# Expert stage of a routed feed-forward kernel: eight hidden chunks between ScalarE and VectorE, results scattered by halves, products of two-expert tiles laid between another tile's long ones

## The chip, the cores and the metric

One core of one Trainium2 chip runs the whole program. The metric is the device time of one execution in microseconds (us). The kernel before was timed in three runs: 1258.9, 1256.6 and 1252.9 us, median 1256.6 us.

## The reference, cut to what matters

The input is 2 images of 256 channels, 56 by 56 pixels, so 6272 tokens of 256 numbers. First comes neighbourhood attention, which this change does not touch. Then every token goes through two of eight experts:

```python
t = _to_tokens(x)
# t + ffn(layernorm(t))
gate_logits = xf @ Wg + bg
top_w, top_i = jax.lax.top_k(gate_logits, 2)
top_w = softmax(top_w)
for e in range(8):
    h = gelu(xf @ W1[e] + b1[e])          # 256 -> 1024, exact gelu
    out = out + w_dense[:, e:e+1] * (h @ W2[e] + b2[e])   # 1024 -> 256
```

So there are 12544 pairs of token and expert, each with a product of 256 by 1024, a gelu, a product of 1024 by 256, a bias, a weight (the gate), and a sum into the output row of the token.

## The kernel before, in words

Stages before the experts compute the attention, the layer norm and the routing, and write every token's normalised row (as two float16 halves of a float32 number, with its output row number and its gate numbers behind) into an expert-sorted table `slots` in HBM. The weights W1 and W2 lie in SBUF as float16 pairs (high part and rest), `w1s` and `w2s`.

The expert stage (`stage_e`) works through NT = 53 tiles of ST = 256 rows. Tiles 0 to 45 and 50 to 52 belong to one expert each. Tiles 46 to 49 (`halves`) are two half tiles of HT = 128 rows, with an expert for each half. Tiles 0 to 43 (`LOOPED` = 44, four tiles a turn, U = 4) run in a loop on each engine, the rest is written out. All engines follow their own program and meet by semaphores:

- **SyncE** (L1493 to L1516) loads the rows of tile m into `xg[m % 4]`, one transfer of 273 KB (two for a tile of halves). From tile 4 on it waits for `xg_free`.
- **TensorE** (L1578 to L1676) has three steps. `turn(m)` transposes the 256 rows of tile m by eight matmuls of 128 columns into `ps_x`, and waits for the load of the tile. `up(m)` makes the eight chunks (HC = 8) of 128 hidden units: six matmuls each with 256 columns, because of the two parts of row and weight. Chunk hc goes to `ps_h[hc % 4]`. `up_halves(m)` does the same for tiles 46 to 49 with twelve matmuls of 128 columns a chunk, six for each half. `down(m)` makes the result of each half of the rows from all eight chunks: 24 matmuls of 256 columns for half 0 and then 24 for half 1, into `ps_y[m % 2]`. The order is up(m+1), turn(m+2), down(m), and so on.
- **ScalarE** (L1679 to L1697) takes each hidden chunk from `ps_h` through the gelu into `gf[hc % 4]`, float32, and raises `g_ok`. For tiles of halves these are two instructions a chunk, since the bias differs.
- **VectorE** (L1758 to L1790) splits each chunk (`split`): a cast into `g_hi` and a subtraction into `g_lo`, which raises `gs_ok`. Then `take_x(m)` copies the transposed rows from `ps_x` to `xt` (L1751) and makes the differences for the gate (L1754). Then `take_y(m)` moves the result of both halves from PSUM to `y_f` with bias (L1788, L1783). The order is split(n+1), take_x(n+2), take_y(n).
- **GpSimd** (L1519 to L1575) makes the gate (`weigh`, four small instructions, each waited for, L1524 to L1535), and in `send(n)` waits for `yf_ok` (L1540) and for the transfers of the tile before (`y_done`, L1543), raises `xg_free` (L1544), multiplies both halves by the gate (L1546, two instructions of 256 columns), waits for them (L1549), and scatters each half with adding into the output by an indirect DMA of its own (L1554).

What paces TensorE inside `up`: chunk hc may start only when the chunk four before it has been split, so from hc = 4 on it waits for VectorE's work on the same tile:

```python
pe.wait_ge(gs_ok, hc - 3 + (0 if first else HC))
```

Load of tile n+3 waits for the `xg_free` that `send(n)` raises; `turn(n+3)` on TensorE follows `up(n+2)`, which begins just when `down(n)` ends.

Of the kernel before, what the change touches and what calls it, by code (L numbers as in the profile page):

```python
# [6 lines left out]
F32 = mybir.dt.float32  # L7
# [4 lines left out]
ALU = mybir.AluOpType  # L12
# [1411 lines left out]
def stage_e(nc, slots_dram, out, w1s, w2s, keep, tc, cf):  # L1424


    with ExitStack() as c:
# [9 lines left out]
        halves = range(PAIR0, PAIR0 + PAIRS)  # L1437
        id_e, b1_sb, b2_sb = keep["id"], keep["b1"], keep["b2"]
# [3 lines left out]
        gf = sb("e_gf", [128, 4, ST], F32)  # L1442
# [25 lines left out]
        xg_f = xg[:, :, :, :].bitcast(F32)  # L1468

# [20 lines left out]
        with nc.Block() as block:  # L1490
# [28 lines left out]
            def _(pool):  # L1519
# [58 lines left out]
            def _(pe):  # L1578
# [11 lines left out]
                def up(m, e, first):  # L1590
# [4 lines left out]
                    for hc in range(HC):  # L1595
                        if not first or hc >= 4:
                            pe.wait_ge(gs_ok, hc - 3 + (0 if first else HC))
                        n = 0
                        for k in range(KC):
                            for w, p in ((0, 0), (0, 1), (1, 0)):  # L1600
                                a = k * FH + hc * 128
                                mm = pe.matmul(ps_h[:, hc % 4, 0:ST],  # L1602
                                               w1s[:, bass.ds(e, 1), w, a:a + 128].rearrange("p a n -> p (a n)"),
# [6 lines left out]
                def up_halves(m, experts):  # L1610
# [3 lines left out]
                    pe.sem_inc(xt_ok, -1)  # L1614
                    for hc in range(HC):
                        pe.wait_ge(gs_ok, hc - 3 + HC)
                        for h, e in enumerate(experts):
                            n = 0
                            for k in range(KC):
                                for w, p in ((0, 0), (0, 1), (1, 0)):  # L1620
                                    a = k * FH + hc * 128
                                    mm = pe.matmul(ps_h[:, hc % 4, h * HT:(h + 1) * HT],
# [4 lines left out]
                    pe.sem_inc(gs_ok, -HC)  # L1627

                def down(m, experts):
                    s = m % 2  # L1630
                    for h in range(2):
                        n = 0
                        for hc in range(HC):
                            for g, w in ((g_hi, 0), (g_hi, 1), (g_lo, 0)):
                                a = hc * C
                                mm = pe.matmul(ps_y[:, s, h * C:(h + 1) * C], g[:, s, hc, h * 128:(h + 1) * 128],  # L1636
                                               w2s[:, bass.ds(experts[h], 1), w, a:a + C].rearrange("p a n -> p (a n)"),
                                               start=n == 0, stop=n == 3 * HC - 1)
                                n += 1
                    mm.then_inc(y_ok, 1)  # L1640
# [10 lines left out]
                with pe.Fori(0, LOOPED // U) as i:  # L1651
                    e = expert(U * i)
                    for j in range(U):
                        after = expert(U * i + j + 1)
                        up(j + 1, after, False)
                        turn(j + 2)
                        down(j, (e, e))
                        e = after
# [3 lines left out]
                for n in range(LOOPED, NT):  # L1662
                    if n + 1 == NT:
                        pe.wait_ge(gs_ok, HC)
                    elif n + 1 in halves:
                        u = 2 * (n + 1 - PAIR0)
                        up_halves(n + 1, (expert_of_half(u), expert_of_half(u + 1)))
                        after = (expert_of_half(u), expert_of_half(u + 1))
                    else:
                        e = expert(n + 1)  # L1670
                        after = (e, e)
                        up(n + 1, e, False)
                    if n + 2 < NT:
                        turn(n + 2)
# [245 lines left out]
```

## Time and profile before

| what | us |
|---|---|
| median of three runs | 1256.6 |
| lowest, highest | 1252.9, 1258.9 |
| span of the profiled execution, first to last instruction | 1258.3 |
| the profiled execution's own time | not given beside the span |
| expert stage, first transpose to the end | 614.0 to 1258.3 |
| of this: tiles in steady order (up of tile 2 begins, up of tile 45 begins) | 639.6 to 1126.4 |
| of this: the four up steps of halves, to the begin of up(50) | 1137.7 to 1201.7 |
| of this: the rest of the products | 1201.7 to 1241.5 |

A row of the timeline reads: start in us, length in us, engine, line of kernel.py, operation, what it writes and what it reads, how many instructions were merged (x), and in brackets how long the engine stood idle before and who released it. PE is TensorE's matmul, PEld its weight load, DVE VectorE, ACT ScalarE, POOL GpSimd, SP SyncE; a q behind the name is the engine's instruction queue. Matmuls overlap in the array, so the length of one (some 0.27 us) is longer than the distance from one to the next. Times are of one profiled execution.

### The profile page before, as it was taken

Reading aid. Unit: us, or ns where it says so; the run is one execution under the profiler, and the core shown is the slowest. Engines: PE = TensorE matmul, PEld = TensorE weight load, DVE = VectorE, ACT = ScalarE, POOL = GpSimd, SP = SyncE. Lnnn points to the kernel's source line nnn. Section 1 sums busy time; section 2 is a strip of 40 time slices with the busy share of each in tenths; the row PEclk is TensorE's granted clock in tenths of the full one; section 3 lists DMA queues with packets and bytes.
Section 4 is the critical chain, followed back from the end, with each engine's and each line's share of the span. In section 5 each row is a group of like instructions: output and inputs, shape, how many; then the busy total and the mean of one; then the engine's idle time right before and its main releaser. Section 6 shows DMA issues by size and latency. Waiting matters only on the chain. (4 is left out here: it accounts for less than half of the span.)

```text
span 1258.3 us, 37927 instructions
## 1 busy us (share of the span) xinstructions
PE 1111.1 (88%) x12025; PEld 947.3 (75%) x12026; DVE 880.8 (70%) x3115; ACT 621.6 (49%) x1315; POOL 727.7 (58%) x786
## 2 busy tenths in 40 slices
PE   4898888989989879972399999999999999999994
PEld 2666678989889868762288888888888888887783
DVE  7887787998989859874366666666676666665452
ACT  4565677988889847651133333333233333333321
POOL 6324255666666617777346566666666666665454
PEclk9999999999999989975699999999999999999998
DMA  7979788778789479986212333223332333323222
GB/s 177 257 232 285 232 216 207 198 192 196 194 197 212 145 238 342 367 293 217 68 28 47 50 43 52 48 48 44 51 51 45 50 44 48 51 48 45 33 40 26
DMA packets 150567, 168.40 MB, mean 134 GB/s; under 512 B 15694, under 2 KB 141694, under 8 KB 150086
## 3 DMA queue, kind: packets, MB, share of 16 engines
q1 hardware_dynamic: 109270, 123.59, 34.7%
q0 software_dynamic: 21984, 31.18, 14.5%
q10 hardware_dynamic: 19232, 12.64, 4.6%
q8 instruction: 40, 0.66, 0.2%
q14 instruction: 41, 0.34, 0.1%
HBM read 107.52 MB, written 64.70 MB: 137 GB/s over the span
## 5 line engine op out<-in xcount | busy, mean ns | idle before, releaser
L1696 ACT ACTIVATE e_gf<-e_ps_h,keep_b 128x256 f32<-128x256 f32 x392 | 185.2, 473 | 366.3 <-PE e_ps_h L1602 366.3
L1602 PE MATMUL e_ps_h<-e_xt,w1s 128*128 128x256 f16 x2352 | 283.3, 276 | 5.1 <-PEq L1594 3.7
L1636 PE MATMUL e_ps_y<-w2s,e_g_hi 128*128 x1696 | 281.9, 273 | 0.0
L1602 PEld LDWEIGHTS e_ps_h<-e_xt,w1s 128*128 x2352 | 217.3, 98 | 64.9 <-issue 33.7
L977 POOL TENSOR_TENSOR b_p<-b_s,b_p 128x392 f16<-128x392 f32 x196 | 178.7, 932 | 96.5 <-DVE b_p L864 82.4
L1636 PE MATMUL e_ps_y<-w2s,e_g_lo 128*128 x848 | 231.8, 273 | 0.0
L1554 POOL DMA_INDIRECT out<-e_y,e_xg x106 | 175.0, 1651 | 83.9 <-POOLq L1549 41.1
L1763 DVE TENSOR_TENSOR e_g_lo<-e_gf,e_g_hi 128x256 f16<-128x256 f32 x424 | 195.3, 461 | 14.6
L1636 PEld LDWEIGHTS e_ps_y<-w2s,e_g_hi 128*128 128x128 f16 x1696 | 164.2, 98 | 18.6
L1761 DVE CAST e_g_hi<-e_gf 128x256 f16<-128x256 f32 x424 | 138.7, 327 | 31.1 <-ACT e_gf L1696 21.3
L923 ACT ACTIVATE b_s<-b_s,b_neg_max 128x196 f32<-128x196 f32 x392 | 159.2, 460 | 0.3 <-DVE b_neg_max L845 0.2
L845 DVE CUSTOM_DVE_ANT_1 b_s<-b_ps_s,bias 128x196 f32<-128x196 f32 x392 | 130.9, 358 | 24.8 <-PE b_ps_s L770 21.0
L1270 POOL DMA_INDIRECT slots<-c_xs,c_slot x98 | 107.5, 1097 | 59.1 <-DVE c_slot L1351 33.2
L1546 POOL TENSOR_SCALAR e_y<-e_y_f,e_gate 128x256 f32<-128x256 f32 x106 | 102.4, 974 | 66.9 <-POOLq L1541 64.4
L954 ACT COPY b_pt<-b_ps_p 98x512 int32<-98x512 int32 x196 | 114.2, 583 | 34.9 <-PE b_ps_p L784 25.9
L1788 DVE SCALAR_TENSOR_TENSOR e_y_f<-e_ps_y,keep_b 128x512 f32<-128x512 f32 x49 | 33.9, 691 | 135.2 <-DVEq L1780 129.7
L784 PE MATMUL b_ps_p<-h_ident,b_p 128*128 128x128 f16 x1568 | 121.5, 221 | 1.7 <-POOL b_p L977 1.0
L802 PE MATMUL b_ps_o<-h_v,b_pt 98*128 98x66 f16 (+1 forms) x2352 | 105.0, 194 | 20.3 <-PEq L795 20.1
L770 PE MATMUL b_ps_s<-h_k,h_q 128*128 128x196 f16 (+1 forms) x784 | 115.0, 270 | 6.9 <-POOL b_p L967 3.0
L802 PEld LDWEIGHTS b_ps_o<-h_v,b_pt 98*128 98x128 f16 x2352 | 91.2, 98 | 22.9 <-issue 22.8
L784 PEld LDWEIGHTS b_ps_p<-h_ident,b_p 128*128 128x128 f16 x1568 | 104.5, 98 | 2.1 <-POOL b_p L977 1.2
L1636 PEld LDWEIGHTS e_ps_y<-w2s,e_g_lo 128*128 128x128 f16 x848 | 83.2, 98 | 9.9
(174 smaller groups left out, 1643.6 us busy)
## 6 DMA issues: line engine op xcount, KB each, us to landing
h_v<-v_rows SPq DMA_DIRECT2D x196, 99.5 KB
e_xg<-slots SPq DMA_DIRECT2D x49, 273.0 KB, 2.8
a_w_in<-in_w SPq DMA_DIRECT2D x16, 512.0 KB, 4.5
c_w_in<-in_w SPq DMA_DIRECT2D x16, 512.0 KB, 8.7
v_rows<-h_v_sb SPq DMA_DIRECT2D x14, 455.0 KB, 7.0
a_x<-in_x SPq DMA_DIRECT2D x14, 448.0 KB, 6.2
qk_hi<-h_o_hi SPq DMA_DIRECT2D x14, 448.0 KB, 4.8
qk_lo<-h_o_lo SPq DMA_DIRECT2D x14, 448.0 KB, 6.7
```

What stands on the lines that cost most here:

```text
L770: mm = pe.matmul(ps_s[:, j % 4, u * KEYS:(u + 1) * KEYS], q[0:rows, s, hp].rearrange("p h (q t) -> p t (h q)", t=COLS)[:, t, :], k[0:rows, ...
L784: last = pe.transpose(ps_p[:, j % 2, m * LANES:(m + 1) * LANES], p16[:, j % RING, half * K2 + u * KEYS + n * CK:][:, 0:128], id_b[:, :])
L802: last = pe.matmul(ps_o[:, n % 2, hp * PVW:hp * PVW + width], pt_sb[:, j % 4, 4 * u + 2 * half + m, :], v_st[:, t, m, at:at + width], star ...
L845: dve.tensor_tensor_reduce(out=s_sb[:, j % RING, u * KEYS:(u + 1) * KEYS].rearrange("p (r w) -> p r w", w=KCOL), in0=ps_s[:, j % 4, u * KE ...
L923: act.activation(p, p, ACT.Exp, bias=neg_max[:, j % RING, u:u + 1], scale=-1.0).then_inc(p_ok, 1)
L977: pool.tensor_tensor(p16[:, m % RING, K2:2 * K2], s_sb[:, m % RING, :], p16[:, m % RING, 0:K2], ALU.subtract).then_inc(lo_ok, 1)
L1554: pool.indirect_dma_start(out=out, out_offset=bass.IndirectOffsetOnAxis(ap=xg[:, j, h, TAIL:TAIL + 1], axis=0), in_=y_sb[:, s, h, :], in_o ...
L1602: mm = pe.matmul(ps_h[:, hc % 4, 0:ST], w1s[:, bass.ds(e, 1), w, a:a + 128].rearrange("p a n -> p (a n)"), xt[:, s, :, 2 * p + k, :], star ...
L1636: mm = pe.matmul(ps_y[:, s, h * C:(h + 1) * C], g[:, s, hc, h * 128:(h + 1) * 128], w2s[:, bass.ds(experts[h], 1), w, a:a + C].rearrange(" ...
L1696: act.activation(gf[:, hc % 4, :], ps_h[:, hc % 4, 0:ST], ACT.Gelu, bias=b1_sb[:, bass.ds(e * HC + hc, 1)], scale=1.0 / WSCALE).then_inc(g ...
L1761: dve.tensor_copy(g_hi[:, s, hc, :], gf[:, hc % 4, :]).then_inc(hi_ok, 1)
L1763: dve.tensor_tensor(g_lo[:, s, hc, :], gf[:, hc % 4, :], g_hi[:, s, hc, :], ALU.subtract).then_inc(gs_ok, 1)
```

## The change

ScalarE's output tile `gf` grows from four to eight chunks. TensorE therefore no longer waits inside `up` for VectorE's split of the same tile, but for ScalarE (`g_ok`) from chunk 4 on; for the first four chunks it still waits for the split of the tile before. VectorE lowers `g_ok` ahead of its last cast. The results of a tile go by halves: `y_ok` is raised for each half, `ps_y` is indexed by the half and no longer by the tile, so `down` first waits for one split chunk of the next tile (`gs_ok`, 1), which in VectorE's order stands behind `take_y` of the tile before. VectorE moves each half by an instruction of its own, GpSimd scales and scatters half 0 and then half 1, and `y_done` is waited for, and `xg_free` raised, behind the scaling of half 0. The last tile puts its results into `ps_h`. In `up_halves`, all eight splits of the tile before are waited for at the beginning, and `down` of the tile before is cut in five parts (10, 10, 10, 9, 9 matmuls), which follow chunks 3 to 7; `turn(n+2)` comes behind all of it and right ahead of the next `up`.

```diff
+        PARTS = (0, 10, 20, 30, 39, 48)
-        gf = sb("e_gf", [128, 4, ST], F32)
+        gf = sb("e_gf", [128, HC, ST], F32)
+        def hidden(hc):
+            return ps_h[:, hc % 4, 0:ST]
+        def result(h, ends):
+            return (ps_h if ends else ps_y)[:, h, 0:C]
...
                 def send(j, n, apart=False):
                     s = j % 2
-                    pool.wait_ge(yf_ok, 1)
-                    pool.sem_inc(yf_ok, -1)
-                    if n is not None:
-                        pool.wait_ge(y_done, 32 * n)
-                        pool.sem_inc(xg_free, 1)
                     for h in range(2):
-                        last = pool.tensor_scalar(y_sb[:, s, h, :], y_f[:, s, h, :], gate[:, j, h:h + 1], None, ALU.mult)
-                    last.then_inc(y_out, 1)
-                    pool.wait_ge(y_out, 1)
-                    pool.sem_inc(y_out, -1)
-                    pool.sem_inc(y_free, 1)
-                    for h in range(2):
+                        pool.wait_ge(yf_ok, 1)
+                        pool.sem_inc(yf_ok, -1)
+                        pool.tensor_scalar(y_sb[:, s, h, :], y_f[:, s, h, :], gate[:, j, h:h + 1], None, ALU.mult
+                                           ).then_inc(y_out, 1)
+                        pool.wait_ge(y_out, 1)
+                        pool.sem_inc(y_out, -1)
+                        if h:
+                            pool.sem_inc(y_free, 1)
+                        elif n is not None:
+                            pool.wait_ge(y_done, 32 * n)
+                            pool.sem_inc(xg_free, 1)
                         if h and apart:
                             pool.wait_ge(y_done, 32 * n + 16)
                         pool.indirect_dma_start(out=out, out_offset=bass.IndirectOffsetOnAxis(
...
                     for hc in range(HC):
-                        if not first or hc >= 4:
-                            pe.wait_ge(gs_ok, hc - 3 + (0 if first else HC))
+                        if hc >= 4:
+                            pe.wait_ge(g_ok, hc - 3)
+                        elif not first:
+                            pe.wait_ge(gs_ok, hc + 5)
...
-                def up_halves(m, experts):
+                def down(m, j, experts, first=0, last=6 * HC):
+                    s = j % 2
+                    if first == 0 and m != NT - 1:
+                        pe.wait_ge(gs_ok, 1)
+                    for i in range(first, last):
+                        h, n = i // (3 * HC), i % (3 * HC)
+                        hc, (g, w) = n // 3, ((g_hi, 0), (g_hi, 1), (g_lo, 0))[n % 3]
+                        a = hc * C
+                        mm = pe.matmul(result(h, m == NT - 1), g[:, s, hc, h * 128:(h + 1) * 128],
+                                       w2s[:, bass.ds(experts[h], 1), w, a:a + C].rearrange("p a n -> p (a n)"),
+                                       start=n == 0, stop=n == 3 * HC - 1)
+                        if n == 3 * HC - 1:
+                            mm.then_inc(y_ok, 1)
+
+                def up_halves(m, experts, now):
                     s = m % 2
                     pe.wait_ge(xt_ok, 1)
                     pe.sem_inc(xt_ok, -1)
+                    pe.wait_ge(gs_ok, HC)
                     for hc in range(HC):
-                        pe.wait_ge(gs_ok, hc - 3 + HC)
+                        if hc >= 4:
+                            pe.wait_ge(g_ok, hc - 3)
...
                         mm.then_inc(h_ok, 1)
-                    pe.sem_inc(gs_ok, -HC)
+                        if hc == 3:
+                            pe.wait_ge(gs_ok, HC + 1)
+                            pe.sem_inc(gs_ok, -HC)
+                        if hc >= 3:
+                            down(m - 1, m - 1, now, PARTS[hc - 3], PARTS[hc - 2])
...
                     elif n + 1 in halves:
                         u = 2 * (n + 1 - PAIR0)
-                        up_halves(n + 1, (expert_of_half(u), expert_of_half(u + 1)))
                         after = (expert_of_half(u), expert_of_half(u + 1))
+                        up_halves(n + 1, after, now)
+                        turn(n + 2)
+                        now = after
...
                 def split(s):
                     for hc in range(HC):
                         dve.wait_ge(g_ok, hc + 1)
-                        dve.tensor_copy(g_hi[:, s, hc, :], gf[:, hc % 4, :]).then_inc(hi_ok, 1)
+                        if hc == HC - 1:
+                            dve.sem_inc(g_ok, -HC)
+                        dve.tensor_copy(g_hi[:, s, hc, :], gf[:, hc, :]).then_inc(hi_ok, 1)
...
+                    for h in range(2):
+                        dve.wait_ge(y_ok, 1)
+                        dve.sem_inc(y_ok, -1)
+                        if not begins and h == 0:
+                            dve.wait_ge(y_free, 1)
+                            dve.sem_inc(y_free, -1)
+                        dve.scalar_tensor_tensor(
+                            y_f[:, s, h], result(h, ends), 1.0 / WSCALE,
+                            b2_sb[:, bass.ds(experts[h], 1), :].rearrange("p a c -> p (a c)"), ALU.mult, ALU.add
+                            ).then_inc(yf_ok, 1)
```

## Rows read from the trace of the kernel before

**Rows 1.** Page, part 1: busy time and share of TensorE's matmuls over the span.
```profile
PE 1111.1 (88%) x12025; PEld 947.3 (75%) x12026; DVE 880.8 (70%) x3115; ACT 621.6 (49%) x1315; POOL 727.7 (58%) x786
```

**Rows 2.** Windows: stretch, its length, busy of PE PEld DVE ACT POOL, clock, DMA.
```profile
639.55:1126.37 486.82, 485.32 (x4474) 407.08 (x4472) 319.63 (x860) 162.61 (x344) 305.98 (x345) 1.00 0.30 48
1137.70:1201.74 64.04, 58.09 (x611) 47.88 (x608) 30.92 (x82) 19.99 (x64) 29.18 (x34) 0.97 0.22 36
1201.74:1230.84 29.10, 28.40 (x258) 22.97 (x256) 19.54 (x54) 10.80 (x23) 16.83 (x19) 1.00 0.25 39
1230.84:1258.30 27.46, 10.64 (x98) 9.30 (x96) 3.11 (x8) 0.57 (x2) 12.44 (x10) 0.77 0.26 29
```

**Rows 3.** Timeline of one steady tile, TensorE: its up step and the weight loads.
```profile
922.96 5.79 PE L1602 MATMUL e_ps_h<-e_xt,w1s 128*128 128x256 f16 x48
922.85 3.26 PEld L1602 LDWEIGHTS e_ps_h<-e_xt,w1s 128*128 x30
926.41 0.55 PEld L1602 LDWEIGHTS e_ps_h<-e_xt,w1s 128*128 x6 [0.29 <-issue]
927.19 0.55 PEld L1602 LDWEIGHTS e_ps_h<-e_xt,w1s 128*128 x6 [0.23 <-issue]
927.92 0.55 PEld L1602 LDWEIGHTS e_ps_h<-e_xt,w1s 128*128 x6 [0.18 <-issue]
```

**Rows 4.** Timeline of the same tile, ScalarE and VectorE.
```profile
923.91 0.47 ACT L1696 ACTIVATE e_gf<-e_ps_h,keep_b 128x256 f32<-128x256 f32 x1 [5.88 <-PE e_ps_h L1602]
924.75 0.58 DVE L1763 TENSOR_TENSOR e_g_lo<-e_gf,e_g_hi 128x256 f16<-128x256 f32 x1
930.01 0.42 DVE L1763 TENSOR_TENSOR e_g_lo<-e_gf,e_g_hi 128x256 f16<-128x256 f32 x1
931.07 0.69 DVE L1751 COPY e_xt<-e_ps_x 128x512 int32<-128x512 int32 x1 [0.63 <-DVEq L1750]
```

**Rows 5.** Timeline of GpSimd: gate of this tile's turn, then the two products.
```profile
932.21 0.19 POOL L1524 TENSOR_TENSOR e_ex<-e_gap 128x2 f32<-128x2 f32 x1 [1.40 <-POOLq L1523]
933.93 0.71 POOL L1533 TENSOR_TENSOR e_gate<-e_ex,e_invert 128x2 f32<-128x2 f32 x1 [0.18 <-POOLq L1532]
935.86 1.90 POOL L1546 TENSOR_SCALAR e_y<-e_y_f,e_gate 128x256 f32<-128x256 f32 x2 [1.22 <-POOLq L1541]
```

**Rows 6.** Timeline: SyncE's loads, and the transposes that waited for one.
```profile
936.59 0.38 SPq L1496 DMA_DIRECT2D e_xg<-slots  x1
733.04 0.38 SPq L1496 DMA_DIRECT2D e_xg<-slots  x1
735.94 0.61 PE L1586 MATMUL e_ps_x<-keep_id,e_xg 128*128 128x128 f16 x8 [0.16 <-PEq L1583]
```

**Rows 7.** First tile of halves: matmuls, queue work by line, ScalarE, VectorE; a window.
```profile
1137.70 8.17 PE L1622 MATMUL e_ps_h<-e_xt,w1s 128*128 128x128 f16 x96
L1622 PEldq FUSED_REGOPS  x64: 46/46/51, 1137.2 to 1145.5; - x64
L1646 PEldq TENSOR_LOAD <-e_half_expert x2: 299/332/366, 1145.8 to 1146.5; - x2
1146.00 0.62 ACT L1689 ACTIVATE e_gf<-e_ps_h,keep_b 128x128 f32<-128x128 f32 x2 [0.42 <-PE e_ps_h L1622]
1148.56 0.69 DVE L1751 COPY e_xt<-e_ps_x 128x512 int32<-128x512 int32 x1 [1.15 <-DVEq L1750]
1194.55:1197.96 3.41, 3.41 (x22) 2.55 (x20) 1.01 (x4) 0.00 (x0) 0.99 (x3) 0.50 0.34 38
```

**Rows 8.** Timeline: transposes of tile 51, then GpSimd at the end.
```profile
1208.18 0.61 PE L1586 MATMUL e_ps_x<-keep_id,e_xg 128*128 128x128 f16 x8 [0.65 <-PEq L1583]
1242.18 1.55 POOL L1554 DMA_INDIRECT out<-e_y,e_xg  x1 [0.30 <-issue]
1246.20 1.82 POOL L1546 TENSOR_SCALAR e_y<-e_y_f,e_gate 128x256 f32<-128x256 f32 x2 [2.47 <-DMA out<-e_y,e_xg]
1253.10 1.56 POOL L1554 DMA_INDIRECT out<-e_y,e_xg  x1 [2.60 <-issue]
```

More of the change, by code:

```diff
@@ L1601, in up @@
                                 a = k * FH + hc * 128
-                                mm = pe.matmul(ps_h[:, hc % 4, 0:ST],
-                                               w1s[:, bass.ds(e, 1), w, a:a + 128].rearrange("p a n -> p (a n)"),
+                                mm = pe.matmul(hidden(hc), w1s[:, bass.ds(e, 1), w, a:a + 128].rearrange("p a n -> p (a n)"),
                                                xt[:, s, :, 2 * p + k, :], start=n == 0, stop=n == 3 * KC - 1)
@@ L1621, in up_halves @@
                                     a = k * FH + hc * 128
-                                    mm = pe.matmul(ps_h[:, hc % 4, h * HT:(h + 1) * HT],
+                                    mm = pe.matmul(hidden(hc)[:, h * HT:(h + 1) * HT],
                                                    w1s[:, bass.ds(e, 1), w, a:a + 128].rearrange("p a n -> p (a n)"),
@@ L1626, in up_halves @@
                         mm.then_inc(h_ok, 1)
-                    pe.sem_inc(gs_ok, -HC)
[L1629 to L1640, printed above, removed]
+                        if hc == 3:
[3 more added lines that the diff above has]
+                            down(m - 1, m - 1, now, PARTS[hc - 3], PARTS[hc - 2])
                 def expert(n):
@@ L1656, in _ @@
                         turn(j + 2)
-                        down(j, (e, e))
+                        down(None, j, (e, e))
                         e = after
@@ L1664, in _ @@
                         pe.wait_ge(gs_ok, HC)
+                        down(n, n, now)
                     elif n + 1 in halves:
                         u = 2 * (n + 1 - PAIR0)
-                        up_halves(n + 1, (expert_of_half(u), expert_of_half(u + 1)))
                         after = (expert_of_half(u), expert_of_half(u + 1))
+                        up_halves(n + 1, after, now)
+                        turn(n + 2)
+                        now = after
                     else:
                         e = expert(n + 1)
-                        after = (e, e)
                         up(n + 1, e, False)
-                    if n + 2 < NT:
-                        turn(n + 2)
-                    down(n, now)
-                    now = after
+                        if n + 2 < NT:
+                            turn(n + 2)
+                        down(n, n, now)
+                        now = (e, e)
             @block.scalar
@@ L1688, in _ @@
                             for h, e in enumerate(experts):
-                                last = act.activation(gf[:, hc % 4, h * HT:(h + 1) * HT], ps_h[:, hc % 4, h * HT:(h + 1) * HT],
+                                last = act.activation(gf[:, hc, h * HT:(h + 1) * HT], hidden(hc)[:, h * HT:(h + 1) * HT],
                                                       ACT.Gelu, bias=b1_sb[:, bass.ds(e * HC + hc, 1)], scale=1.0 / WSCALE)
@@ L1810, in _ @@
                         take_x((n + 2) % U, n + 2, n + 2 in halves)
-                    take_y(n % U, n, False, n in halves)
+                    take_y(n % U, n, False, n in halves, n == NT - 1)
 def col_windows(q):
```

23 lines of the change are left out of this document (4 added, 19 removed).

## The prediction, made before the changed kernel was run

> **What bounds the kernel now.** I read the page first: TensorE is busy 88% of the span [rows 1]. The windows say where it is not: in the 43 steady tiles matmuls run 485.3 of 486.8 us, in the stretch of half tiles 58.1 of 64.0, and after 1230.84 only 10.6 of 27.5 [rows 2]. A busy matmul engine is not one at its peak, so the steady tile is checked against the distance of its instructions. 30 weight loads go in 3.26 us, 0.109 each [rows 3]. So `up` and `down` are worth 48 x 0.109 = 5.23 us each, the eight transposes of half as many columns 0.44, and a tile 10.90. Measured are 486.82 / 43 = 11.32. The missing 0.42 us is in `up`: its 48 matmuls take 5.79 - 0.27 (the length of the last) = 5.52 from first to last start where 47 x 0.109 = 5.12, and the weight loads stop three times, ahead of chunks 5, 6 and 7, for 0.29, 0.23 and 0.18 [rows 3]. These are the waits for VectorE's split. The change takes exactly these away, and the question is what comes next.
>
> **Step 1, waits inside `up`.** From chunk 4 on TensorE waits for ScalarE. ScalarE's first chunk is done 923.91 + 0.47 = 1.42 us after the tile's begin [rows 4]; TensorE wants it at 4 x 0.654 = 2.62. 1.2 us of slack, and both go on at one pace: the wait is gone. Alone this would be worth 0.42 x 43 = 18 us.
>
> **Step 2, the load behind `xg_free`.** `turn(n+3)` needs the load that `send(n)` frees. Before, GpSimd frees it ahead of its products, now behind the product of half 0 and its wait. Let T be the begin of `up` of one tile, 922.96. VectorE's last subtraction ends at 930.43 = T + 7.47, the copy begins at 931.07, the gate at 932.21 and ends at 934.64 = T + 11.68 [rows 4, 5]. None of it is moved by the change: VectorE's chain starts with ScalarE's first chunk and then runs without a pause, and the move of half 0 (half of the old instruction) fits between copy and the end of the gate, since half 0 of `down` ends at about T + 5.7 + 2.6. So half 0 is ready before GpSimd is, and the gate is what `send` waits for. From there: two waits and the start of the product, 0.33 (0.18 for one wait with its start, 0.15 for the further one) [rows 5]; product 1.90 / 2 = 0.95; two waits and the raise, 0.20: `xg_free` at T + 13.16. Before, it came 0.18 ahead of the products, at 935.68 = T + 12.72, and the load was issued 0.91 later, at 936.59 [rows 5, 6]. From issue to the transposes are 735.94 - 733.04 = 2.90 us where they waited for it [rows 6]. So the transposes can begin at T + 13.16 + 0.91 + 2.90 = T + 16.97. TensorE without waits would be there at T + 10.90 + 5.23 = T + 16.13. It is 0.84 us early. A stall s ahead of `turn` lengthens the tile and also delays the next demand, so 2s = 0.84, s = 0.42, and the tile takes 10.90 + 0.42 = 11.32 us: what it takes now. The waits inside `up` turn into one wait ahead of `turn`, and the steady stretch gains nothing.
>
> Bounds: the transfer now begins beside the scatter of half 0, which is issued at about the same moment; before, the scatter came 2 us later. From issue to use lies between 2.90 and the 4.02 us that a scatter takes from issue to the product waiting for it [rows 8]; each 0.1 us is worth 0.05 a tile, 2.1 us in all. I take 3.0: +2. If VectorE's chain were 0.7 shorter (all of its subtractions 0.42 and never 0.58 [rows 4]), s would be near 0.05, -16.
>
> **Step 3, the half tiles.** Before, a period is four steps: 96 short matmuls, first to last start 8.17 - 0.23 = 7.94 us, held up by 64 register instructions of the queue in 8.3 us; two loads of the expert numbers into TensorE's registers, some 1.5 us with the array idle; transposes; `down` [rows 7]. 64.04 us from up(46) to up(50) [rows 2]. Now the second pair of register loads is gone and `down` lies between chunks. A chunk of shorts alone costs 1.0 us (three of them, 3.0). A chunk with ten long ones lies between 12 x 0.054 + 10 x 0.109 = 1.74 (the array) and 1.0 + 1.09 = 2.09; the queue gains ahead during the long ones, for which it needs 0.083 each like for the short ones and not 0.109, so I take 1.9: four of them 7.6, and 0.8 for the shorts of the last: the last short starts some 11.5 us after the first. What was hidden before now stands open: `turn(n+2)` is followed by the `up` that needs its copy. Before, 0.36 us after the last short ScalarE starts (1146.00 against 1145.64), and the copy begins at 1148.56, 2.92 after it, held up by VectorE's own register loads (1.15 idle), and takes 0.69 [rows 7]. With 0.4 for the wait and the first matmul the next `up` starts 4.0 after the last short. Of these only 1.4 are covered by nine long ones and the transposes, so TensorE stands still for 2.6 us three times, and some 2.0 ahead of up(50), whose tile has one expert to load. Sum: 3 x 15.5 + 14.9 = 61.4, which is 2.6 less than before. The stretch holds one interval of 3.41 us at a granted clock of 0.50, the level of 1.2 GHz, 22 matmuls [rows 7]; I leave one in. Each further one costs 0.4 (in shorts, which the queue holds anyway) to 1.7 us. Range of the step: -6 to +5.
>
> The Trainium skill says (TensorE: Matmul & The Clock Gate, "What's actually happening") that the throttled clock is the default and activity releases it. By that the new pauses speak against the change; the trace has a fall right behind such a stretch once and none behind the three earlier ones.
>
> **Step 4, tiles 50 to 52.** The load for `turn(51)` waits for `send(48)`, whose results VectorE can move only after the late copy. With the copy ending 0.4 ahead of up(50), the gate ends 0.45 + 2.43 later (its lengths above), at +2.5; then 1.48 + 0.91 + 2.90: transposes at +7.8, where they now stand at 1208.18 - 1201.74 = 6.44 [rows 8]: +1.35. The next two `up` lose their 0.4 each: -0.8. Sum +0.6.
>
> **Step 5, the end.** Before, the products of tile 52 wait for the last scatter of tile 51, issued at 1242.18: 1246.20; two products (1.82) and 0.88 later the first scatter, then the second, which waits for the first (1253.10), then 5.2 us to the end [rows 8]. Now half 0 of both tiles is scaled while TensorE works on half 1. In tile 51 the product of half 1 and its scatter follow when half 0's scatter is issued, about 9.3 us after 1230.84 against 11.3: -2.0. In tile 52 the product of half 0 is finished before the wait ends: -1.9. Sum -3.9, between -1.9 (tile 51 no earlier) and -6. The last scatter's wait stays.
>
> **Step 6**, costed at nothing: the wait for one split chunk ahead of `down` (it came at T + 2 and `down` begins at T + 6; were it late, all transposed work behind it would be); the wait for all eight splits ahead of `up_halves` (1.8 us earlier than the copy's end); two result moves instead of one on VectorE (it has 2.8 us of idle there); one result tile per half, since VectorE has long moved the old one.
>
> **The sum.** 0 + 2 - 2.6 + 0.6 - 3.9 = -3.9 us against the profiled span of 1258.3, which lies 1.7 above the median of the runs. I apply the difference to the median: 1252.7 us.
>
> **Rivals.** *A, the load is in time.* Then TensorE runs at 10.9 to 11.1: -10 to -18 for the steady stretch, 1236 to 1245. For it: before, only one wait for a load shows in the rows, and 0.84 us of lateness is a sum of ten lengths. Against: both ends of that chain are in program order. Chance 0.18. *B, the load is slower still.* It shares the DMA engines with the scatter that now starts with it. At 3.6 us instead of 2.9, s = 0.77, the tile 11.67, +15: 1265; with halved clock in the half tiles 1268. It decides above 3.2 us from issue to use, where the steady stretch loses more than the rest brings. For it: half 0's scatter is issued 0.1 us from the load. Against: 48 GB/s and a DMA share of 0.30 leave room [rows 2]. Chance 0.17. *C, products and splits block each other.* The product of half 1 now falls between splits. The rows show 0.58 for a subtraction beside a product and 0.42 alone [rows 4], 0.16 and not the product's 0.95. If the product of half 1 held back VectorE whole, its chain would end 0.8 later, s + 0.4, +17: 1270. Chance 0.03. The Trainium skill (SBUF — State Buffer, "SBUF: two separate sides") states that lock: a VectorE operation with two SBUF inputs and a GpSimd operation reading SBUF exclude each other for a whole instruction. The rows do not bear that out. *D, the half tiles do not gain:* every period 1.5 us longer, with two more halved intervals: +8 against the sum, 1260. Chance 0.12.
>
> **How the numbers follow.** Forecast 0.50 (1248 to 1257), A 0.18, B 0.17, C 0.03, D 0.12. What differs from 1256.6 by less than 0.5%, 6.3 us, can't be told from no change: 1250.3 to 1262.9. Faster: A and a fifth of the forecast, 0.29. Slower: B nearly whole and C, 0.19. Same: 0.52. The range 1241 to 1266 leaves out some 0.07 of A, 0.08 of B and C.
>
> **What would show it.** In the changed trace: no idle in PEld ahead of chunks 5 to 7; instead PE idle ahead of the transposes, 0.4 us in nearly every tile, released by the load; load issues some 14.1 us after their T; period 11.3. Idle of 2.6 us ahead of up(47), up(48), up(49). The last scatter at about 1249. It would be wrong if PE showed no idle ahead of the transposes (A) or over 0.6 us (B).

## The result

The changed kernel takes 1262.6 us (median of 10 runs, 1260.0 to 1267.7) where the kernel before took 1256.8 (10 runs): ratio 1.0043, interval 1.0023 to 1.0063. Timed again on another chip it was 1.0030 (1.0006 to 1.0054). The forecast was 1252.7, with a chance of 0.50 for 1248 to 1257. The time lies outside that, inside the full range of 1241 to 1266, and the direction was wrong. In its profiled execution the span is 1258.3 us and the time 1260.2, so 1.9 us lie around the span. The span of the kernel before was the same, 1258.3. If the same 1.9 us lie around it, that execution was some 3 us above its median, twice as far as the prediction had put it.

One pair of traces was too little to find 5 us: the stages ahead of the experts, which the change does not touch, scatter by 3 to 7 us between executions on one chip. So the stretches below are means over all traces of each kernel (4 of before, 5 of the changed one), in us. `up(45)` in the table stands for the begin of that step:

| stretch | before | changed | difference | forecast |
|---|---|---|---|---|
| first transpose to up(2) | 25.4 | 25.0 | -0.5 | 0 |
| up(2) to up(45), 43 tiles | 486.7 | 493.2 | +6.5 | +2 |
| up(45) to up(46) | 11.4 | 12.8 | +1.4 | 0 |
| up(46) to up(50) | 64.6 | 61.9 | -2.7 | -2.6 |
| up(50) to the last two down steps | 29.2 | 31.5 | +2.3 | +0.6 |
| from there to the end | 27.4 | 23.4 | -4.0 | -3.9 |
| expert stage | 644.7 | 647.8 | +3.1 | -3.9 |

The expert stages of the changed kernel range from 643.7 to 650.8, so the standard error of 3.1 is some 1.4 us, and 3.1 does not contradict the 5.4 and 3.8 us of the timed runs. The traces are not spread evenly over the chips: where both kernels were profiled side by side (the first pair, e7 and e8, f1 to f4), the changed stage is longer by 1.7, by -0.6 and by 5.3 us. The row of the half tiles hangs on one trace: three of before's take 64.0 us and one (f3) 66.1, so against the usual one the gain is 2.2.

### The profile page after: what moved, and what is told of

The parts are those of the page before. It is cut to its first block and busy times, and to the rows that moved or that the text cites. A ratio compares the mean times of both kernels' runs of the same rounds, so it can differ in the third digit from the quotient of the medians.

```text
span 1258.3 us, 38111 instructions
## 1 busy us (share of the span) xinstructions
PE 1094.1 (87%) x12025; PEld 961.1 (76%) x12026; DVE 900.7 (72%) x3164; ACT 621.4 (49%) x1315; POOL 741.6 (59%) x786
## 5 line engine op out<-in xcount | busy, mean ns | idle before, releaser
L1629 PE MATMUL e_ps_y<-w2s,e_g_hi 128*128 x1664 | 277.7, 273 | 0.1
L1613 PE MATMUL e_ps_h<-e_xt,w1s 128*128 128x256 f16 x2352 | 267.5, 274 | 6.6 <-PEq L1603 6.2
L1613 PEld LDWEIGHTS e_ps_h<-e_xt,w1s 128*128 x2352 | 230.2, 98 | 37.8 <-issue 10.0
L1629 PE MATMUL e_ps_y<-w2s,e_g_lo 128*128 x832 | 227.2, 273 | 0.0
L1785 DVE TENSOR_TENSOR e_g_lo<-e_gf,e_g_hi 128x256 f16<-128x256 f32 x424 | 202.4, 477 | 14.6
L1783 DVE CAST e_g_hi<-e_gf 128x256 f16<-128x256 f32 x424 | 144.8, 342 | 63.6 <-ACT e_gf L1716 41.8
L1629 PEld LDWEIGHTS e_ps_y<-w2s,e_g_hi 128*128 128x128 f16 x1664 | 161.0, 98 | 18.7
L1552 POOL TENSOR_SCALAR e_y<-e_y_f,e_gate 128x256 f32<-128x256 f32 x106 | 146.1, 1378 | 16.2 <-POOLq L1551 13.8
L845 DVE CUSTOM_DVE_ANT_1 b_s<-b_ps_s,bias 128x196 f32<-128x196 f32 x392 | 130.8, 358 | 25.8 <-PE b_ps_s L770 22.3
L954 ACT COPY b_pt<-b_ps_p 98x512 int32<-98x512 int32 x196 | 114.3, 583 | 35.3 <-PE b_ps_p L784 27.7
L1804 DVE SCALAR_TENSOR_TENSOR e_y_f<-e_ps_y,keep_b 128x256 f32<-128x256 f32 x104 | 43.8, 424 | 104.8 <-DVEq L1800 75.9
```

What stands on the lines that cost most here:

```text
L845: dve.tensor_tensor_reduce(out=s_sb[:, j % RING, u * KEYS:(u + 1) * KEYS].rearrange("p (r w) -> p r w", w=KCOL), in0=ps_s[:, j % 4, u * KE ...
L1613: mm = pe.matmul(hidden(hc), w1s[:, bass.ds(e, 1), w, a:a + 128].rearrange("p a n -> p (a n)"), xt[:, s, :, 2 * p + k, :], start=n == 0, s ...
L1629: mm = pe.matmul(result(h, m == NT - 1), g[:, s, hc, h * 128:(h + 1) * 128], w2s[:, bass.ds(experts[h], 1), w, a:a + C].rearrange("p a n - ...
L1783: dve.tensor_copy(g_hi[:, s, hc, :], gf[:, hc, :]).then_inc(hi_ok, 1)
L1785: dve.tensor_tensor(g_lo[:, s, hc, :], gf[:, hc, :], g_hi[:, s, hc, :], ALU.subtract).then_inc(gs_ok, 1)
```

## The profile after

The windows of the changed kernel's first trace, cut at the same steps as [rows 2]; columns: stretch, length, busy of PE, PEld, DVE, ACT, POOL, clock, DMA share, GB/s.

```profile
636.89:1128.69 491.80, 476.66 (x4474) 419.79 (x4472) 337.22 (x903) 162.63 (x344) 318.36 (x344) 1.00 0.29 47
1141.89:1203.42 61.53, 52.57 (x611) 45.95 (x608) 32.38 (x83) 19.99 (x64) 26.37 (x28) 0.97 0.23 37
1203.42:1234.89 31.47, 28.57 (x256) 25.14 (x257) 19.96 (x54) 10.77 (x23) 19.85 (x23) 0.95 0.22 36
1234.89:1258.30 23.41, 10.65 (x98) 9.30 (x95) 4.21 (x11) 0.60 (x2) 12.38 (x10) 0.79 0.30 35
```

The steady tiles take 491.80 / 43 = 11.44 us, and now matmuls are busy in only 476.7 of 491.8 us. In [rows 2] it was 485.3 of 486.8: the old waits were so short that overlapping matmuls hid them from the busy time, the new one is long enough to show. The list of waits over that stretch says where (who waited, for whom, us in total, times, longest):

```profile
PEld e_ps_x L1595 <- issue: 22.3, 31, 1.1
PE e_ps_x L1595 <- PEq L1592: 14.4, 28, 0.9
PEld e_ps_h L1613 <- issue: 3.3, 10, 0.4
```

The third row was 27.1 us in 109 stops before: the waits inside `up` are gone. The first two rows are one wait, that of the transposes for the load, as the weight loads and as the matmuls see it, so they are not to be added. From the last start of `up` to the first transpose it lengthens the tile by 0.46 us on average. It is not even: in many pairs of tiles one waits and the next does not, as the transposes of four tiles in a row show:

```profile
699.60 0.61 PE L1595 MATMUL e_ps_x<-keep_id,e_xg 128*128 128x128 f16 x8
711.55 0.61 PE L1595 MATMUL e_ps_x<-keep_id,e_xg 128*128 128x128 f16 x8 [0.86 <-PEq L1592]
722.68 0.61 PE L1595 MATMUL e_ps_x<-keep_id,e_xg 128*128 128x128 f16 x8
734.47 0.61 PE L1595 MATMUL e_ps_x<-keep_id,e_xg 128*128 128x128 f16 x8 [0.70 <-PEq L1592]
```

The lateness fixes only the sum of two waits that follow each other (the prediction's 2s), not how it is shared. One tile with its neighbours, timeline, answers to [rows 3 to 6]:

```profile
854.40 5.41 PE L1613 MATMUL e_ps_h<-e_xt,w1s 128*128 128x256 f16 x48
861.91 0.43 DVE L1785 TENSOR_TENSOR e_g_lo<-e_gf,e_g_hi 128x256 f16<-128x256 f32 x1
862.87 0.69 DVE L1771 COPY e_xt<-e_ps_x 128x512 int32<-128x512 int32 x1 [0.54 <-DVEq L1770]
865.74 0.71 POOL L1542 TENSOR_TENSOR e_gate<-e_ex,e_invert 128x2 f32<-128x2 f32 x1 [0.18 <-POOLq L1541]
865.80 5.23 PEld L1613 LDWEIGHTS e_ps_h<-e_xt,w1s 128*128 x48
866.75 0.94 POOL L1552 TENSOR_SCALAR e_y<-e_y_f,e_gate 128x256 f32<-128x256 f32 x1 [0.30 <-DVE e_y_f L1804]
868.67 1.79 POOL L1563 DMA_INDIRECT out<-e_y,e_xg  x1 [0.99 <-POOLq L1551]
868.79 0.38 SPq L1505 DMA_DIRECT2D e_xg<-slots  x1
869.19 0.75 DVE L1785 TENSOR_TENSOR e_g_lo<-e_gf,e_g_hi 128x256 f16<-128x256 f32 x1
869.95 1.94 POOL L1552 TENSOR_SCALAR e_y<-e_y_f,e_gate 128x256 f32<-128x256 f32 x1
871.64 0.55 PE L1595 MATMUL e_ps_x<-keep_id,e_xg 128*128 128x128 f16 x7 [0.33 <-PEq L1592]
```

The reader sees 48 weight loads in 5.23 us without a stop; the gate ending at 866.45 = T + 12.05 (T, the begin of `up`, is 854.40); the product of half 0 ahead of the load's issue at T + 14.39; and the transposes 2.85 us behind that issue, at T + 17.24. The next `up` began at 865.90 and was finished with its 5.24 us at 871.14: TensorE waits 0.5 us. The subtraction beside the scatter takes 0.75 us (0.43 at 861.91), and the product of half 1 is recorded as 1.94 us where the first takes 0.94: it starts while the scatter is still being issued (868.67 to 870.46).

Around the half tiles and at the end:

```profile
1131.93 1.47 SPq L1525 DMA_DIRECT2D e_xg<-slots  x2
1136.21 0.61 PE L1595 MATMUL e_ps_x<-keep_id,e_xg 128*128 128x128 f16 x8 [2.12 <-PEq L1592]
1152.40 0.83 PE L1649 MATMUL e_ps_h<-e_xt,w1s 128*128 128x128 f16 x12
1156.30 0.69 DVE L1771 COPY e_xt<-e_ps_x 128x512 int32<-128x512 int32 x1 [1.04 <-DVEq L1770]
1157.29 0.86 PE L1649 MATMUL e_ps_h<-e_xt,w1s 128*128 128x128 f16 x9 [2.62 <-PEq L1639]
1206.59 1.19 POOL L1552 TENSOR_SCALAR e_y<-e_y_f,e_gate 128x256 f32<-128x256 f32 x1 [0.30 <-POOLq L1551]
1211.73 1.01 PE L1595 MATMUL e_ps_x<-keep_id,e_xg 128*128 128x128 f16 x8 [2.90 <-PEq L1592]
1253.24 1.58 POOL L1563 DMA_INDIRECT out<-e_y,e_xg  x1 [1.74 <-issue]
```

The transposes of tile 46 wait 2.1 us: its load is two transfers, the second issued 1.1 us after the first. Behind `up_halves(46)` stand the forecast 2.6 us of pause for the copy (1156.30, then 1157.29). The product of tile 48's half 0 (1206.59) is what the load of tile 51 now stands behind: its transposes come 8.3 us after `up(50)` begins (forecast 7.8, before 6.4), after a pause of 2.90 us. That pause is followed by an interval at a granted clock of 0.50, the level of 1.2 GHz, that did not fall there before:

```profile
1211.70:1214.40 2.70, 2.67 (x17) 2.19 (x18) 0.96 (x3) 0.00 (x0) 1.28 (x2) 0.50 0.17 27
```

`down(49)` takes 6.20 us where 5.24 is usual. Four of the five traces of the changed kernel have this interval and take 31.5 to 31.8 us for the stretch; e8 has a pause of 2.79 us in the same place and no such interval, and takes 30.7. None of the four traces of before has it. The Trainium skill (TensorE: Matmul & The Clock Gate, "What's actually happening") says that the throttled clock is the default and activity releases it. The four falls behind this pause agree with that, and e8 shows that the pause alone does not decide it.

## The experiments

Times of different chips differ (before: 1256.8, 1281.8, 1278.4 us on three), so each ratio is against the kernel before run on the same chip. "Stage" is the expert stage in the profile, from the first transpose to the end.

**e1: `xg_free` ahead of the product again**, and with it the wait for `y_done`, all else as changed.

```diff
                         pool.sem_inc(yf_ok, -1)
+                        if h == 0 and n is not None:
+                            pool.wait_ge(y_done, 32 * n)
+                            pool.sem_inc(xg_free, 1)
                         pool.tensor_scalar(...)
...
-                        elif n is not None:
-                            pool.wait_ge(y_done, 32 * n)
-                            pool.sem_inc(xg_free, 1)
```

> The changed kernel, with one thing moved: send() waits for y_done and raises xg_free ahead of the product of half 0, as before, and not behind it. Theory L (the load of tile n+3 is late because xg_free is raised one product later): xg_free comes 1.14 us earlier in the chain, 16.97 falls to 15.8 us against a demand at 16.13, the wait ahead of the transposes (mean 0.47 us a tile in the changed kernel) goes, a steady tile takes 10.95 to 11.05 us where it takes 11.44, and the program 1240 to 1244 us (about 20 less than the changed kernel's 1262.6, ratio to the kernel before about 0.988). Rival R (what costs is GpSimd's product beside VectorE's splits, which makes VectorE's chain 0.26 us longer): that product stays where it is, so a tile keeps 11.3 us or more and the program 1258 or more.

Measured: ratio 0.9865 (0.9827 to 0.9903); tile 475.29 / 43 = 11.05 us; stage 629.1. The window, and then the row of the waits that was 14.4 us (its twin of the weight loads went from 22.3 to 2.6):

```profile
662.77:1138.06 475.29, 472.51 (x4474) 421.56 (x4472) 339.74 (x903) 162.62 (x344) 315.50 (x344) 1.00 0.30 49
```

```profile
PE e_ps_x L1595 <- PEq L1592: 1.2, 4, 0.3
```

Three moved lines turn 0.4% slower into 1.35% faster. GpSimd's product beside the splits stayed (some 1.4 us on average, as in the changed kernel), VectorE's last subtraction still ends at T + 7.8, and neither cost anything any more: rival R falls as a cause of its own.

**e2: the eight chunks alone**, in the kernel before.

```diff
-        gf = sb("e_gf", [128, 4, ST], F32)
+        gf = sb("e_gf", [128, HC, ST], F32)
...
-                        if not first or hc >= 4:
-                            pe.wait_ge(gs_ok, hc - 3 + (0 if first else HC))
+                        if hc >= 4:
+                            pe.wait_ge(g_ok, hc - 3)
+                        elif not first:
+                            pe.wait_ge(gs_ok, hc + 5)
```

> The kernel before, with the eight chunks of gf and the g_ok waits alone; results whole, half tiles and end as before. Theory L: xg_free stays ahead of the products at T + 1.40 of the next tile, plus 0.91 and 2.90 makes 5.21 us where TensorE wants the tile at 5.23: the load is just in time, a tile takes 10.95 to 11.1 us instead of 11.32, the program 1243 to 1247 us, ratio about 0.99. Rival (taking the split waits out of up is worth nothing by itself, since the load binds right behind them): 11.25 or more a tile, within 3 us of the kernel before.

Measured: 0.9906 (0.9877 to 0.9935), stage 628.7, and the tile from the window:

```profile
664.33:1139.29 474.96, 472.80 (x4475) 421.07 (x4473) 320.45 (x860) 162.62 (x344) 304.91 (x345) 1.00 0.30 49
```

474.96 / 43 = 11.05 us. So this part of the change is worth 12 us in the steady stretch and was eaten by the other part. e1, with results by halves and the early `xg_free`, takes 11.05 as well: the halves cost nothing there as long as the load is early.

**e3: the halves alone**: gf of four chunks and the old waits, half tiles' steps in the old order, the rest of the change kept.

```diff
-        gf = sb("e_gf", [128, HC, ST], F32)
+        gf = sb("e_gf", [128, 4, ST], F32)
...
-                        if hc >= 4:
-                            pe.wait_ge(g_ok, hc - 3)
-                        elif not first:
-                            pe.wait_ge(gs_ok, hc + 5)
+                        if not first or hc >= 4:
+                            pe.wait_ge(gs_ok, hc - 3 + (0 if first else HC))
```

> The changed kernel with gf of four chunks and the gs_ok waits of before, and the half tiles' steps in the order of before: what is left is the results by halves alone. Theory L: TensorE loses its 0.4 us inside up and still wants the tile at 16.9, the load gives it at 17.2, so a further 0.1 to 0.2 us wait ahead of the transposes and 11.4 to 11.5 us a tile, +4 to +7 us on the steady stretch, -4 at the end: 1257 to 1261 us. If the halves cost nothing in the steady stretch: 11.32 a tile and 1252 to 1254.

Measured: 1.0040 (1.0016 to 1.0063), tile 11.53, a little over the expected 11.4 to 11.5; last stretch 22.8. The same loss as the whole change: the waits are 0.24 us ahead of the transposes and the old 0.31 in `up`, and they add up to much the same period, which the load sets.

**e4: no interleaving of the half tiles.**

```diff
-                        if hc == 3:
-                            pe.wait_ge(gs_ok, HC + 1)
-                            pe.sem_inc(gs_ok, -HC)
-                        if hc >= 3:
-                            down(m - 1, m - 1, now, PARTS[hc - 3], PARTS[hc - 2])
+                    pe.sem_inc(gs_ok, -HC)
...
-                        after = (expert_of_half(u), expert_of_half(u + 1))
-                        up_halves(n + 1, after, now)
+                        up_halves(n + 1, (expert_of_half(u), expert_of_half(u + 1)), now)
+                        after = (expert_of_half(u), expert_of_half(u + 1))
                         turn(n + 2)
+                        down(n, n, now)
```

> The changed kernel with the half tiles' steps one after the other as before (up_halves, transposes, down), all else as changed. By the windows of the two traces the interleaving saved 2.5 us from up(46) to up(50) and made the stretch behind it 2.4 us longer (the late copy ahead of up(50), the late load for the transposes of tile 51). So the sum should be near nothing: 1261 to 1265 us beside the changed kernel's 1262.6. If the interleaving were a gain of its own, the time would be 1266 or more; if it were the reason for the loss, 1258 or less.

Measured: 0.9998 (0.9974 to 1.0021), stage 644.8. From up(46) to up(50) it takes 63.9 us (61.9 with interleaving), behind it 27.7 (31.5): the interleaving loses about 2 us in sum. Its interval and the changed kernel's first one just miss each other, but lie on different chips, and the changed kernel's second one (1.0006 to 1.0054) overlaps it. By the mark that I had set (1258 or less) the interleaving would be the reason for the loss, since 0.9998 of 1256.8 is 1256.5; the traces give it only those 2 us. With the load early it costs nothing that the traces show: these two stretches take 91.6 us in e1, which interleaves, and 92.0 in b1 below, which does not. How much of the loss is its share stays open between nothing and some 5 us; e1 to e3 do not hang on it.

**e5: the load issued later**, a dose for the law s = half of the delay.

```diff
-                    row = sp.value_load(row_no[0:1, bass.ds(n, 1)], min_val=0, max_val=ROWS - ST)
+                    for _ in range(3):
+                        row = sp.value_load(row_no[0:1, bass.ds(n, 1)], min_val=0, max_val=ROWS - ST)
```

> The changed kernel; SyncE reads the row number of the tile three times instead of once ahead of each load, which by its trace (0.65 us from one read to the next) issues every load 1.3 us later, and nothing else is touched. Theory L: a delay in the chain xg_free - load - transposes lengthens the tile by half of it, since the next demand is delayed as well: 11.44 + 0.65 = 12.1 us a steady tile, +28 us on the 43, and a wait of 1.1 to 1.2 us ahead of the transposes (now 0.47). Rival (the load is not what TensorE waits for, or the wait is not shared by the demand): unchanged 11.4, or 11.44 + 1.3 = 12.7.

Measured in one run: 1326.2 us; the window of the 43 tiles:

```profile
664.51:1194.56 530.05, 481.48 (x4474) 420.94 (x4472) 333.78 (x903) 162.97 (x344) 316.56 (x345) 0.99 0.26 44
```

A tile takes 530.05 / 43 = 12.33 us, +0.89. The reads made the load 1.2 us later, and from issue to transposes it now took 3.4 us instead of 2.9. The packets of the two transfers show why. On average over the steady tiles of the changed kernel, the load's packets end 2.46 us after its issue and the first of the scatter come at 2.25, so they hardly meet; here the scatter's come at 1.79 and the load's end at 2.93. Together 1.7 us of delay, half 0.85. In this one run the law holds and my dose was off: the delayed transfer also became slower, which is rival B's mechanism. At the change's own timing it is next to absent: from issue to use are 2.93 us on average, 3.03 in f2 and 3.02 in f4.

**e6, e7, e8 and f1 to f4: the same two kernels again**, for the scatter of single traces.

> The changed kernel itself once more, on the chip of this call, as the yardstick for the other kernels here and for a second trace. Same ratio to the kernel before as in the result, 1.002 to 1.006; steady tiles of 11.44 us; the profile's stretches of the expert stage within 0.5 us of the first trace. If the ratio is 1.000 or below, the interleaving of the half tiles (which without it measured 0.9998) is not what costs.

> The kernel before, one profiled execution on the chip of this call, to be laid stretch by stretch beside the changed kernel on the same chip. Theory (all of the loss lies in the expert stage and the two first profiles differed by chance before it): from the first transpose to the end 641 to 644 us, steady tiles of 11.32, 27.5 us from the last pair of down steps to the end.

> The changed kernel, one profiled execution on the same chip. Theory: the stages ahead of the experts equal to e7's within 1.5 us, the expert stage 646 to 649 us, 3 to 6 us longer than e7's; steady tiles of 11.44. Rival (the change also costs ahead of the expert stage, by the larger gf or otherwise): the first transpose over 2 us later than in e7.

> The kernel before, a further profiled execution; with f2 to f4 on one chip. Theory (stages ahead of the experts vary by some us from execution to execution, the same in both kernels): first transpose anywhere within 6 us of f3's; expert stage 643.5 to 645 us.

> The changed kernel, a further profiled execution. Theory: expert stage 643.5 to 649 us, its spread coming from the load of tile 46 (11.4 to 15.0 us between up(45) and up(46) so far) and tile 51; first transpose as scattered as in f1 and f3. Rival (it costs ahead of the experts): first transpose over 3 us later than both f1's and f3's.

> The kernel before, its second profiled execution on this chip. Theory as for f1: first transpose within 6 us of f1's, expert stage 643.5 to 645 us.

> The changed kernel, its second profiled execution on this chip. Theory as for f2: expert stage 643.5 to 649 us, first transpose as scattered as before's. Rival: over 3 us later than both of before's.

| run | before | changed | | before | changed | changed |
|---|---|---|---|---|---|---|
| | e7 | e8 | e6 | f1, f3 | f2 | f4 |
| first transpose at | 607.6 | 613.3 | 631.9 | 636.4, 640.7 | 637.2 | 639.8 |
| steady tile | 11.32 | 11.43 | 11.43 | 11.31, 11.32 | 11.53 | 11.52 |
| stage | 644.2 | 643.7 | 648.5 | 644.2, 645.9 | 650.8 | 649.8 |

e8 was off both ways: the first transpose came 5.7 us after e7's and the stage was no longer than e7's. f1 to f4 settle it: ahead of the experts the changed kernel lies between the two of before, so that is scatter. Other expectations were missed too. e7 is 0.2 us over its 644. e6 had to be within 0.5 us of the first trace in each stretch and has 15.0 us from up(45) to up(46) where that has 13.2, with a halved clock inside. f3 is 0.9 us over its 645, by two more intervals of halved clock in the half tiles than the other traces of before. f2 and f4 missed the top of my range (649) by 1 to 2 us: the steady tile itself is 0.1 us longer there, with some 0.55 us of wait. The kernel before takes 11.31 to 11.32 on every chip; why the changed one differs is open.

**b1 and b2: better versions.** b1 is e4 with `xg_free` raised early while a load still waits for it (and late in the last three tiles, where the late wait shortens the end). b2 has the same early `xg_free` and interleaves, but puts `turn(m + 1)` behind chunk 5 of `up_halves(m)`, lets VectorE take the rows ahead of its last two splits, and waits for the old splits chunk by chunk:

```diff
-                    pe.wait_ge(gs_ok, HC)
                     for hc in range(HC):
                         if hc >= 4:
                             pe.wait_ge(g_ok, hc - 3)
+                        else:
+                            pe.wait_ge(gs_ok, hc + 5)
...
                             down(m - 1, m - 1, now, PARTS[hc - 3], PARTS[hc - 2])
+                        if hc == 5:
+                            turn(m + 1)
...
-                def split(s):
+                def split(s, take=None):
                     for hc in range(HC):
+                        if hc == 6 and take is not None:
+                            take_x(*take)
```

> The parts that measured well, together: eight chunks, results by halves, half tiles' steps one after the other as before, xg_free raised ahead of the product while a load still waits for it (n + 3 < NT), and behind it for the last three tiles. Sum from the stretches of the traces so far, from the first transpose: 25.4 + 43 x 11.05 + 11.3 + 62.5 + 27.5 + 22.6 = 624 us against 644 before, 20 less: ratio 0.984. If halves and early xg_free get in each other's way (GpSimd's product of half 1 beside the splits makes VectorE's chain longer): tiles of 11.2 or more, ratio 0.989 or above.

> As b1, but with the half tiles interleaved as in the changed kernel and the pause behind them taken away: turn(n+2) stands behind chunk 5 of up_halves, VectorE takes the transposed rows ahead of its last two splits, and up_halves waits for the splits of the tile before chunk by chunk. Theory (the pause of 2.0 to 2.7 us ahead of each up step behind a half tile is the copy left open by the interleaving): no pause over 0.5 us, 13.0 us a period instead of 15.5, from up(46) to up(50) 52 to 54 us instead of 61.5, and 616 us for the expert stage, ratio 0.978. If the queue's register work paces this stretch anyway: 58 or more and a ratio like b1's.

Measured: b1 0.9851 (0.9817 to 0.9886), stage 625.2, tile 11.04. b2 0.9798 (0.9764 to 0.9833), stage 615.8. The windows of b2, cut like those above:

```profile
662.73:1137.23 474.50, 472.38 (x4474) 421.68 (x4472) 339.51 (x903) 162.63 (x344) 314.45 (x344) 1.00 0.30 49
1148.47:1202.73 54.26, 51.80 (x611) 44.41 (x608) 32.13 (x83) 19.98 (x64) 31.10 (x34) 1.00 0.26 42
1202.73:1231.42 28.69, 27.41 (x256) 24.24 (x257) 20.22 (x55) 10.77 (x23) 18.47 (x20) 1.00 0.27 42
1231.42:1253.60 22.18, 10.65 (x98) 9.29 (x95) 3.93 (x11) 0.59 (x2) 11.76 (x9) 0.79 0.28 33
```

The half tiles take 54.3 us instead of 61.9 (expected 52 to 54), at full clock throughout. Its matmuls never stand still for more than 1.0 us there, where the changed kernel has pauses of 2.62, 2.15, 2.21 and 1.86: not the 0.5 that I expected, but most of the pause is gone. That fits the copy left open behind the interleaving as what made it worthless; b2 changes three things at once, so their shares are not shown. b2 is 2.0% faster than the kernel before and the fastest that I ran; its interval and b1's overlap by a little.

## Why the prediction was right and wrong

The step that failed is step 2: its term of +2 us for the steady stretch measured +6.5. The mechanism was right, two sizes in it were off. Two terms that the prediction put at nothing came on top, tile 46's load and the clock behind the load of tile 51.

- **Step 1 (waits inside `up` go, worth 18 us alone)**: right in kind; e2 shows 486.7 - 475.0 = 11.7 us in the steady stretch. The size was too large. From first to last start `up` takes 5.45 us on average before and 5.13 in e2, so the waits were worth 0.31 us a tile and not 0.42. The tile without any wait is not 10.90 but 10.98: the distances, rounded to 0.109, add up short, and at the loop's end, once in four tiles, `down` is followed by a further 0.2 us. A few late loads make 11.05 of it in e2.
- **Step 2 (the load behind `xg_free` eats the gain)**: the mechanism is shown by e1, e2 and e5 from three sides. It failed in its numbers, in two places. It added the wait to a tile of 10.90 us where 10.98 is right. And it took VectorE's chain as unmoved ("None of it is moved by the change"). Before, the last subtraction ends at T + 7.53 on average, in the changed kernel at T + 7.72 to 7.85, because scatter and product now run beside other splits (up to 0.75 us for a subtraction beside the scatter's issue). That this comes from the halves is shown by e2 (whole results, 7.55) against e1 and e3 (halves, 7.84 and 7.79). The median end of the gate moves from T + 11.69 to T + 11.89 in the first trace. So the transposes can begin at T + 17.12 to 17.34, 17.22 on average, where the sum has 16.97 and, with its 3.0 us for the load, 17.07. Each of the two errors counts by half: 0.04 and 0.07 us a tile. In 43 tiles that is 4.9 us, against the 4.5 that lie between +2 and +6.5. Tile 11.43 to 11.53 instead of 11.37. That the wait itself came out as forecast (0.42 and a little, measured 0.46) is in part luck: a later load lengthens it and a longer tile shortens it. It was to show in nearly every tile; it shows in some three of four and often alternates.
- **Step 3 (half tiles -2.6)**: -2.7, with the pause of 2.6 us in place behind `up_halves(46)` and 1.9 to 2.2 behind the others. Without f3 it is -2.2. The prediction left one interval of halved clock in; the changed kernel's traces have one to three. f3, with three, takes 2.1 us more than the other traces of before, with one each. Not seen in the step: the transposes of tile 46, whose load is two transfers, wait for the same chain (+1.4, the clock of e6 in it).
- **Step 4 (+0.6)**: +2.3. The late load came as forecast (8.3 against 7.8 us); the clock halved behind it in four of five traces, which I had left out here.
- **Step 5 (-3.9)**: -4.0, with the last scatter issued at 1253.24 in a stretch that began 4 us later.
- **Sum**: -3.9 forecast, +3.1 in the traces, +5.4 in the timed runs. Of the 7.0 us, 4.5 are step 2's, 1.4 tile 46, 1.7 step 4, and -0.6 the rest. The remaining 2.3 us between traces and timed runs lie within the scatter of both; where they fall is not shown.
- **Rivals**: A is excluded by the waits and D by the stretch itself. C had VectorE's chain 0.8 us later; its last subtraction came 0.2 to 0.3 later, which is part of step 2, and e1 shows that this costs nothing once the load is early. B names the right direction, but its condition, over 3.2 us from issue to use, was not met (2.93 to 3.03). A's time does not follow from its parts: 10 to 18 us off the steady stretch and the other steps' -5.9 give 1233 to 1241 and not 1236 to 1245; e1, where the load is in time, has a ratio that would be 1240 here.
- The sum is a difference from a profiled execution whose own time lay some 3 us above the median, and not 1.7 as I wrote. The difference was applied to the median, so the sign does not hang on it.

## What to carry to other kernels

A wait that is removed from the busiest engine may only uncover the next one. Before trusting the gain, walk the loop's other ring (here result, gate, free, load, transpose) and write both arrivals with tenths of a us. Where a release stands in program order matters more than the work around it: an early "free" that needs no result must stay ahead of the instruction that does. And when products are laid between others to fill gaps, ask which copy had been hidden behind them.

## What was not expected of the hardware

- In this ring of buffers, once its load is what TensorE waits for, a further delay lengthens the tile by half of it: 1.7 us gave 0.89, in one run.
- The wait for such a load is not the same in every tile: 0.86 us, none, 0.70, none.
- A GpSimd product that starts while an indirect scatter is still being issued is recorded with 1.5 to 2.0 us, otherwise with 0.96 on average; VectorE's subtraction beside the scatter's issue takes up to 0.75 instead of 0.42.
- The kernel before took 1256.8, 1281.8 and 1278.4 us (medians) on three chips. In the traces the difference lies ahead of the expert stage: the first transpose comes at 608 to 614 us in the session of the result and that of e7 and e8, and at 631 to 642 in the others. Why is open; the expert stage of one kernel agrees within 2 us for before and 7 us for the changed one.
